# Softmax probabilities multiplied by inverted row sums on GpSimd, ahead of transposes that run two rounds behind the scores

## What is computed

```python
h = layernorm(x) * (1 + ca) + sa
x = x + ga * attention(h)      # 16 heads of 64
h = layernorm(x) * (1 + cb) + sb
x = x + gb * experts(h)        # 160 experts of 64, 8 kept per token, and a shared one

# attention, for each batch and head
scores = q @ k.T / 8 + bias          # 512 x 512, bias by relative position
attn = softmax(scores, axis=-1)
a = attn @ v
y = concat(a over heads) @ o_w.T
```

## Time and profile before

| what | value |
|---|---|
| median of 3 runs | 1040.71 us (1038.21 to 1040.87) |
| profiled execution: its time, its span | 1039.4 us, 1037.6 us |
| TensorE matmuls busy | 974.3 us, 94% |
| VectorE, ScalarE, GpSimd busy | 770.4 us (74%), 696.6 us (67%), 20.0 us (2%) |
| exponentials on ScalarE (L747) | 256, 718 ns each |
| biased scores on VectorE (L1028) | 256, 688 ns each |

### The profile page before, as it was taken

One profiled execution on the slowest core, in us unless ns is written; L12 is line 12 of the kernel. 1 busy time (PEld: TensorE's weight loads), 2 busy tenths in 40 slices (PEclk: granted clock), 3 DMA queues, 4 the chain that ended last, 5 costly groups with the idle time before them and its releaser, 6 DMA issues.

```text
span 1037.6 us, 16983 instructions
## 1 busy us (share of the span) xinstructions
PE 974.3 (94%) x4720; PEld 704.8 (68%) x4720; DVE 770.4 (74%) x1356; ACT 696.6 (67%) x1200; POOL 20.0 (2%) x36
## 2 busy tenths in 40 slices
PE   4899999999999999999978699999999999999997
PEld 2565656566666666666643487888888888888886
DVE  5766656566566665666655488999999999999997
ACT  4556656566665666666645567777777777777775
POOL 0000000000000000000000000000000000000000
PEclk9999999999999999999998899999999999999999
DMA  7874353443543534534500499999999999999992
GB/s 211 270 200 107 80 140 82 103 108 80 137 106 78 122 88 115 122 82 102 122 21 1 135 219 221 220 218 220 219 217 222 219 219 219 220 218 221 219 219 66
DMA packets 71106, 160.49 MB, mean 155 GB/s; under 512 B 10272, under 2 KB 36192, under 8 KB 60944
## 3 DMA queue, kind: packets, MB, share of 16 engines
q1 hardware_dynamic: 71056, 159.97, 68.3%
HBM read 105.60 MB, written 2.42 MB: 104 GB/s over the span
## 4 chain that ended last, share of the span: by engine, by line
PE 86%; ACT 4%; DMA 3%; DVE 3%; issue 2%; SPq 2%; DVEq 0%; ACTq 0%
PE ps L658 41%; PE ps L466 11%; PE ps L451 9%; PE ps L434 5%; PE ps L436 5%; PE ps L408 4%; PE ps L419 2%; PE ps L487 2%; PE ps L479 2%; ACT r_sb L762 2%; DMA k_low<-qk 1%; DMA hcur<-hT 1%; SPq L298 1%; DMA comb_rows<-strips 1%; PE ps L576 1%
## 5 line engine op out<-in xcount | busy, mean ns | idle before, releaser
L747 ACT ACTIVATE prob<-s_sb,nmax 128x512 f32<-128x512 f32 x256 | 183.6, 718 | 114.1 <-DVE nmax L1028 113.5
L658 PE MATMUL ps<-hT,wT 128*128 128x512 f32 x960 | 244.6, 391 | 0.3 <-DVE wT L1191 0.3
L1210 DVE TENSOR_TENSOR PT<-v_sb,strips 128x1024 f32<-128x1024 f32 x160 | 195.8, 1224 | 43.2 <-ACT v_sb L879 29.7
L658 PEld LDWEIGHTS ps<-hT,wT 128*128 128x128 f32 x960 | 180.8, 189 | 39.1 <-ACT strips L854 1.1
L658 PE MATMUL ps<-stack,wT 128*128 128x512 f32 x640 | 198.3, 392 | 9.0 <-DVE wT L1197 9.0
L879 ACT ACTIVATE v_sb<-ps 128x1024 f32<-128x1024 f32 x160 | 164.4, 1028 | 60.1 <-PE ps L658 59.8
L229 DVE COPY PT<-ps 128x512 f32<-128x512 f32 x128 | 88.3, 690 | 145.2 <-PE ps L451 145.0
L1197 DVE TENSOR_TENSOR wT<-PT,stack 128x1024 fp32r<-128x1024 f32 x160 | 194.8, 1218 | 0.0
L871 ACT CAST stack<-PT 128x1024 fp32r<-128x1024 f32 x160 | 166.7, 1042 | 9.0 <-DVE PT L1210 9.0
L1028 DVE CUSTOM_DVE_ANT_0 s_sb<-ps,strips 128x512 f32<-128x512 f32 x256 | 166.8, 688 | 6.6 <-PE ps L436 6.5
L451 PE MATMUL ps<-ident,prob 128*128 128x128 f32 x1024 | 140.9, 275 | 12.0 <-ACT r_sb L762 8.7
(11 more groups left out here) (108 smaller groups left out, 758.4 us busy)
## 6 DMA issues: line engine op xcount, KB each, us to landing
strips<-comb_rows SPq DMA_DIRECT2D x158, 512.0 KB, 13.2
stack<-qk SPq DMA_DIRECT2D x128, 256.0 KB, 3.8
k_low<-qk SPq DMA_DIRECT2D x64, 128.0 KB, 3.7
hT<-qk SPq DMA_DIRECT2D x64, 128.0 KB, 3.7
strips<-bias_rows SPq DMA_DIRECT2D x3, 1792.0 KB, 10.2
strips<-in_L_ffn_w_gate SPq DMA_DIRECT2D x80, 64.0 KB, 11.6
strips<-in_L_ffn_w_down SPq DMA_DIRECT2D x80, 64.0 KB, 13.6
strips<-bias_rows SPq DMA_DIRECT2D x2, 896.0 KB, 5.2
```

Source lines behind the costliest of these rows:

```text
L658: last = nc.tensor.matmul(ps[:, bank + c, :], weights(a), rows(m, c), start=start and k == 0, stop=stop and k == 2, skip_group_check=True)
L747: nc.scalar.activation(prob[:, u % 4, :], s_sb[:, u % 2, :], ACT.Exp, bias=nmax[:, u % 4:u % 4 + 1], scale=-1.0, accum_out=rsum[:, n % 2, ...
L1210: nc.vector.tensor_tensor(weighted[:, k % 4, :], silu[:, k % 2, :], cb[:, r, half * HALF:(half + 1) * HALF], ALU.mult).then_inc(s_mul, 1)
```

## The change

- The sums are used on the probabilities. `invert_sums` runs for two units at a time (four times a pair), and GpSimd's new `normalise` multiplies each unit's prob in place by its column of rinv. `widen_sums`, `spread_sums`, `copy_sums`, r_sb and rinv_wide are gone. VectorE's multiply behind attend becomes `copy_o`, a plain copy.
- prob has eight buffers, one for each unit; `add_bias` writes its result there and `exponential` works in place. s_sb is gone.
- The transposes of two units stand two rounds behind their scores. `attend` for a pair, `project_out`, `project_v` and the copies move accordingly. `qk_high` and `qk_low` of pair n+2 now stand in round 3 of pair n, in front of the next pair's operations.
- Without the sums' transposes the two banks alternate with the unit's number, and `transpose_users` is gone.

```diff
-            def transpose_probs(b, n, u, final):
-                pe.wait_ge(s_exp, b * G + (UNITS * n + u + 1))
-                bank = bank_for(b, ("T", n, u), final)
+            def transpose_probs(b, n, u):
+                g = UNITS * n + u
+                pe.wait_ge(s_prob, b * G + (g + 1))
+                if g >= 2:
+                    pe.wait_ge(*copied(b, g - 2))
                 for kb in range(QT):
-                    last = nc.tensor.transpose(ps[:, bank, kb * P:(kb + 1) * P],
-                                               prob[:, u % 4, kb * P:(kb + 1) * P], ident[:, :])
+                    last = nc.tensor.transpose(ps[:, BANK_T + u % 2, kb * P:(kb + 1) * P],
+                                               prob[:, u, kb * P:(kb + 1) * P], ident[:, :])
                 last.then_inc(s_t, 1)
...
-            def spread_sums(b, n, final):
-
-                pe.wait_ge(s_wide, b * HPAIRS + (n + 1))
-                bank = bank_for(b, ("R", n, 0), final)
-                for qt in range(QT):
-                    last = nc.tensor.transpose(ps[:, bank, qt * P:(qt + 1) * P], rinv_wide[:, qt, :], ident[:, :])
-                last.then_inc(s_t, 1)
-
...
                 scores(b, n, 0)
                 scores(b, n, 1)
                 if n >= 2:
-                    project_out(b, n - 2)
+                    attend(b, n - 2, 2)
+                    attend(b, n - 2, 3)
                 if n == 0:
                     project_qk(b, 1)
                 if n >= 1:
-                    transpose_probs(b, n - 1, 6, final)
-                    transpose_probs(b, n - 1, 7, final)
+                    transpose_probs(b, n - 1, 4)
+                    transpose_probs(b, n - 1, 5)
 
                 scores(b, n, 2)
                 scores(b, n, 3)
-                if n >= 1:
-                    attend(b, n - 1, 0, final)
-                    attend(b, n - 1, 1, final)
-                    spread_sums(b, n - 1, final)
-                transpose_probs(b, n, 0, final)
-                transpose_probs(b, n, 1, final)
-
-                scores(b, n, 4)
-                scores(b, n, 5)
-                if n >= 1:
-                    attend(b, n - 1, 2, final)
-                    attend(b, n - 1, 3, final)
                 if n == 0:
                     project_v(b, 0)
                 if not (final and n >= HPAIRS - 1):
                     project_v(b, n + 1)
-                transpose_probs(b, n, 2, final)
-                transpose_probs(b, n, 3, final)
+                if n >= 2:
+                    project_out(b, n - 2)
+                if n >= 1:
+                    transpose_probs(b, n - 1, 6)
+                    transpose_probs(b, n - 1, 7)
+
+                scores(b, n, 4)
+                scores(b, n, 5)
+                if n >= 1:
+                    attend(b, n - 1, 0)
+                    attend(b, n - 1, 1)
+                transpose_probs(b, n, 0)
+                transpose_probs(b, n, 1)
 
                 scores(b, n, 6)
                 scores(b, n, 7)
@@ -533,8 +492,8 @@
                     transpose_y(b)
                 if not (final and n >= HPAIRS - 2):
                     project_qk(b, n + 2)
-                transpose_probs(b, n, 4, final)
-                transpose_probs(b, n, 5, final)
+                transpose_probs(b, n, 2)
+                transpose_probs(b, n, 3)
...
-                if n >= 1 or u >= 4:
-                    number, _, _ = tables[False][1]["T", n - (u < 4), (u + 4) % UNITS]
-                    act.wait_ge(s_t, b * NU + (number + 1))
-                nc.scalar.activation(prob[:, u % 4, :], s_sb[:, u % 2, :], ACT.Exp, bias=nmax[:, u % 4:u % 4 + 1],
-                                     scale=-1.0, accum_out=rsum[:, n % 2, u:u + 1]).then_inc(s_exp, 1)
+                nc.scalar.activation(prob[:, u, :], prob[:, u, :], ACT.Exp, bias=nmax[:, u:u + 1],
+                                     scale=-1.0, accum_out=rsum[:, u:u + 1]).then_inc(s_exp, 1)
 
             def copy_probs(b, n, u):
-                number, _, _ = tables[False][1]["T", n, u]
-                act.wait_ge(s_t, b * NU + (number + 1))
-                if u == ACT_COPIES[0] and n >= 2:
+                act.wait_ge(s_t, b * G + (UNITS * n + u + 1))
+                if u == 0 and n >= 2:
                     act.wait_ge(s_pv, b * HPAIRS + (n - 1))
...
             def pair(b, n, final=False):
 
+                exponential(b, n, 0)
+                exponential(b, n, 1)
+                if n == 0:
+                    qk_high(b, 1)
                 if n >= 1:
                     copy_probs(b, n - 1, 4)
-                exponential(b, n, 0)
-                exponential(b, n, 1)
+
+                exponential(b, n, 2)
+                exponential(b, n, 3)
+                if n == 0:
+                    copy_v(b, 0)
+                if not (final and n >= HPAIRS - 1):
+                    copy_v(b, n + 1)
                 if n >= 1:
                     copy_probs(b, n - 1, 6)
-                if not (final and n >= HPAIRS - 1):
-                    qk_high(b, n + 1)
-
-                exponential(b, n, 2)
-                if n >= 1:
-                    copy_sums(b, n - 1, final)
-                exponential(b, n, 3)
-
-                copy_probs(b, n, 0)
+
                 exponential(b, n, 4)
                 exponential(b, n, 5)
                 if n == 0:
-                    copy_v(b, 0)
                     first_high(2)
                     first_high(3)
-                if not (final and n >= HPAIRS - 1):
-                    copy_v(b, n + 1)
-
-                copy_probs(b, n, 2)
+                copy_probs(b, n, 0)
+
                 exponential(b, n, 6)
                 exponential(b, n, 7)
+                if not (final and n >= HPAIRS - 2):
+                    qk_high(b, n + 2)
+                copy_probs(b, n, 2)
...
-            def widen_sums(b, n):
-
-                pool.wait_ge(s_rinv, b * HPAIRS + (n + 1))
-                if n >= 1:
-                    number, _, _ = tables[False][1]["R", n - 1, 0]
-                    pool.wait_ge(s_t, b * NU + (number + 1))
-                pool.sem_inc(apart, 1)
-                nc.gpsimd.tensor_copy(rinv_wide[:, :, :].rearrange("p q (h d) -> p q h d", h=2),
-                                      rinv[:, n % 2, :].rearrange("p (h q o) -> p q h o", h=2, o=1).broadcast_to(
-                                          [P, QT, 2, HD])).then_inc(s_wide, 1)
-
-            widen_sums(0, 0)
-            with pool.Fori(0, B - 1) as b:
-                for n in range(1, HPAIRS + 1):
-                    widen_sums(b, n)
-            for n in range(1, HPAIRS):
-                widen_sums(B - 1, n)
+            def normalise(b, n, u):
+
+                if u % 2 == 0:
+                    pool.wait_ge(s_rinv, b * (G // 2) + (UNITS * n + u) // 2 + 1)
+                    pool.sem_inc(apart, 1)
+                nc.gpsimd.tensor_scalar(prob[:, u, :], prob[:, u, :], rinv[:, u:u + 1], None,
+                                        ALU.mult).then_inc(s_prob, 1)
+
+            with pool.Fori(0, B) as b:
+                for n in range(HPAIRS):
+                    for u in range(UNITS):
+                        normalise(b, n, u)
...
                 g = UNITS * n + u
                 dve.wait_ge(s_s, b * G + (g + 1))
-                if g >= 2:
-                    dve.wait_ge(s_exp, b * G + (g - 1))
+                if g == UNITS - 1:
+                    dve.wait_ge(grp_used, 2)
+                if n >= 1:
+                    dve.wait_ge(s_t, b * G + (g - UNITS + 1))
                 dve.sem_inc(apart, 1)
                 if u == 0 and 2 * n in STRIP_PARTS:
                     dve.wait_ge(ld[f"strips{STRIP_PARTS.index(2 * n)}"], 16)
                 at = strip3[:, 2 * (n % HPAIRS) + head, qt * P:qt * P + S]
                 backwards = bass.AP(at.tensor, at.offset + S - 1, [list(at.ap[0]), [-1, S]])
-                nc.vector.tensor_tensor_reduce(out=s_sb[:, u % 2, :], in0=ps[:, BANK_S + u % 2, :],
+                nc.vector.tensor_tensor_reduce(out=prob[:, u, :], in0=ps[:, BANK_S + u % 2, :],
                                                in1=backwards, scale=-1.0, scalar=3.0e38,
                                                op0=ALU.add, op1=ALU.min,
-                                               accum_out=nmax[:, u % 4:u % 4 + 1]).then_inc(s_ttr, 1)
+                                               accum_out=nmax[:, u:u + 1]).then_inc(s_ttr, 1)
 
             def copy_probs(b, n, u):
-                number, _, _ = tables[False][1]["T", n, u]
-                dve.wait_ge(s_t, b * NU + (number + 1))
+                dve.wait_ge(s_t, b * G + (UNITS * n + u + 1))
                 if u == 1 and n >= 2:
                     dve.wait_ge(s_pv, b * HPAIRS + (n - 1))
-                copy_unit(nc.vector.tensor_copy, n, u, number).then_inc(s_cd, 1)
-
-            def invert_sums(b, n):
-                dve.wait_ge(s_exp, b * G + UNITS * (n + 1))
```

(55 more changed lines are left out.)

82 lines of the change are left out of this document (25 added, 57 removed).

## The result

The changed kernel took 1014.8 us in the median (1013.8 to 1015.6, four runs), the kernel before 1040.8 beside it: a ratio of 0.976 with an interval of 0.974 to 0.977, 26 us less. The forecast was 1013, so the total came out within 2 us. It did so by luck, with terms that missed in both directions, and the multiply, which was priced without a row, cost more than its upper bound. TensorE's matmuls are busy for 953.2 us (94%), VectorE 769.4 (76%), ScalarE 679.4 (67%), GpSimd 398.1 (39%, it was 2%).

A forecast was written before the change was run, and what follows sets the result against it. TensorE was taken to bound the attention stage, pair by pair. From the profiled 1039.4 us, 27.0 (pairs) and 8.1 (DMAs) off and 7.2 (seams) back gave 1011.5, or 1013 against the median; range 999 to 1030.

The forecast's parts named there:

- TensorE sets the pair: In the attention stage TensorE's work sets the time, one pair of heads at a time, 32 times, 15.27 us each before.
- R: TensorE's transposes of the widened sums; removing them and the wait they bring was priced at 1.04 us a pair.
- A's new wait of 0.4: In each pair the first attend waits about 0.4 us for ScalarE's copy of probabilities, making a pair 14.4 us.
- the rival of TensorE's full pace: In the attention stage attend's wait vanishes or ScalarE comes early enough: a pair at 14.0, 1001 us, chance 0.14.
- The 0.23 read as a wait: In each pair of the kernel before, TensorE was taken to wait 0.23 us before the first attend.
- The multiply at 1.0 between 0.62 and 1.23: GpSimd's multiply of 128x512 was priced at 1.0 us, bounds 0.62 and 1.23; eight a pair, 8.0 us, hidden behind TensorE.
- The slow-multiply rival: GpSimd's multiplies set the pair if each takes 1.8 us or more; at 2.0 the time is 1055 us, chance 0.12.
- hcur: In the attention stage TensorE's waits for the load of hcur go: 4.8 us, plus 1.7 us of slow clock.
- k_low: In the attention stage TensorE's 1.6 us wait for a stack's DMA goes, as qk_low moves about two rounds earlier.
- the head: The first pairs of the attention stage, whose extra cost was left at nothing.
- The seams: At three seams between batches, longer waits behind VectorE's queue and a slower clock give back 7.2 us together.
- The end: The tail behind the last scores was left at nothing: more work there but fewer waits.

The follow-up runs named there:

- sums_free: The kernel before in its old order, without widening, transposes and copy of the sums or the multiply by them, so without the division: 1014.3 us, ratio 0.978.
- cheap_pool: The changed kernel with GpSimd's multiply replaced by a copy in place, so without the division by the sums: 1013.6 us, ratio 0.973.
- lag_one: The changed kernel with transposes one round behind their scores, engine orders shifted to match, reciprocals right behind the biased scores: 1098.3 us, ratio 1.055.
- strips_late: The changed kernel with bias strips 3 and 4 loaded one stack later each: four runs of 1011.0, 1016.9, 1031.4 and 1034.3 us, no ratio.

## Why the prediction came out right

**TensorE sets the pair: right.** Taking R out was worth 1.03 in sums_free, priced at 1.04; the parts behind this agree less well (see there).

**A's new wait of 0.4: wrong, 6.7 us too pessimistic over 28 pairs.** The chain was followed with each record's full duration, but records of one engine overlap a little. ScalarE in the changed kernel, round 1 and 2 of the pair whose scores start at 228.73:

```profile
234.94 0.71 ACT L706 ACTIVATE prob<-prob,nmax 128x512 f32<-128x512 f32 x1
235.55 0.19 ACT L706 ACTIVATION_READ_ACCUMULATOR prob<-prob,nmax 128x1 f32 x1
235.64 0.56 ACT L719 COPY v_sb<-ps 128x512 f32<-128x512 f32 x1
236.11 0.58 ACT L204 COPY PT<-ps 128x512 f32<-128x512 f32 x1
```

copy_v starts at 6.91 behind the pair's start where I had 7.25, and it takes 0.47 from start to start, not 0.55. The copy of unit 6 ends at 7.96 instead of 8.3, and A starts at 8.27, which is 1.10 behind its S, the distance that it has without any wait. qk_high, likewise, was 0.90 in pace (228.65 to 229.55) against 1.01 in length, and a reciprocal 0.07 against the 0.20 charged for it. From the 14.01 of the prediction to the 14.17 measured it is then 0.09 more for S in front of each A, 0.05 more for T behind each A and 0.10 less for v, which took 0.71 instead of 0.81. No wait is in it: for the pair the rival of TensorE's full pace came true, and the forecast's step of a late copy in front of A failed. The 0.23 read as a wait in the kernel before was likewise 0.13, since 1.10 is the bare distance.

**The multiply at 1.0 between 0.62 and 1.23: the price was wrong, its cover right.** It is 1.56. The bounds came from the engine's own copy, 0.62, and twice that; the product with a scalar from memory is 2.5 copies. The slow-multiply rival needed 1.8 to decide; the real margin was 0.2 us an operation (14.17 over 8 is 1.77), not the 0.8 that the forecast gave itself. Of the rivals I had given this one 0.12, which the price turned out nearly to earn. The two rounds of lag made latency free in the steady pairs (cheap_pool, lag_one), though not in the tail (see the end, below).
The estimate from the Trainium skill (GPSIMD Engine Reference, "Performance versus the Vector engine"), 1.35 us, was nearer than mine and still low. The page's ratio was measured on an add of two tiles, not on a product with a column. Against VectorE on the same operands in SBUF the ratio measured here is 1.56 to 0.48, 3.2 and not 1.96.

**hcur: right.** 6.6 us against 6.5, and sums_free shows that it was the order that removed it, since without the new order the waits grew from 4.8 to 8.5. The forecast asked for both moves, and lag_one bears it out: with qk_low early but `project_v` in its old round, SP waits up to 6.1 us for `project_v` and the matmuls wait 4.2 us for hcur.

**k_low: wrong, and the head with it.** The 1.6 us wait was to go, because qk_low comes two rounds earlier. SP does issue pair 2's stack 3.8 us earlier (46.04, before 49.88), but its transfers share the DMA engines with two strips of 1.8 MB issued in front of them and land no earlier, while TensorE arrives sooner (at 59.0, before 60.6). The wait is now 3.8. strips_late shows the cause: with the second of them behind the stack the wait is gone and pairs 1 and 2 take 3.2 less. The whole stretch up to pair 3 missed its forecast by 5.4 us. Of this 1.0 lies in front of the first scores, which start at 29.4 (before 28.4, and 28.0 to 29.4 in the other profiles with the same order in the attention); its cause is open.

**The seams: right in kind, 2.6 us too small.** TensorE's waits were 4.5 where 4.1 was forecast, for the jump took 3.88 on VectorE and not the 2.73 of the earlier trace rows; part of the difference was absorbed, since VectorE came to it 3.9 us behind the pair's start and not 4.2. I had taken idle time measured in one order as the price of the jump; how much of it is a fixed cost no row of before could tell. The clock fell behind both waits. Beside the waits 3.0 and 2.1 us are left (7.5 and 6.6 less 4.5) against 1.7 each; the granted clock of 0.52 and 0.69 over 5.5 us stands for 2.6 and 1.7 of them. The third seam, without a jump, cost 1.5 against 1.4. By the rule of the Trainium skill (TensorE: Matmul & The Clock Gate, "What's actually happening") a wait of this length need not be caught; here both were, 0.52 and 0.69 in the windows shown.

**The end: 1.1 us longer, forecast at nothing.** The tail of the attention is what grew. From the start of pair 31 to the last `project_out` it was 21.7 us before (540.07 less 518.33) and is 23.9 now (515.61 less 491.68); with the copy in cheap_pool it is 22.3. So 1.6 of these 2.2 us are the multiply, which has no round of scores to hide behind there:

```profile
509.68 0.65 PE L420 MATMUL ps<-ident,prob 128*128 128x128 f32 x4 [0.88 <-POOL prob L859]
```

The prediction gave the tail "more work behind the last scores but fewer waits"; the waits were not fewer, 2.5 us of TensorE's up to the last `project_out` against 2.0 before. The stages behind the tail were about 1 us shorter in this profile, which the edit doesn't explain.

**The sum** was right since +6.7 for the pairs met -2.6, -5.4 and -1.1 for seams, head and end. Each of these four is a miss of its own, and that their balance, 2.3 us, is small is luck.

## What to carry to other kernels

Follow a chain across engines by start-to-start differences of records, not by their durations: 0.1 us at each of four steps was the whole forecast wait. An operation on an idle engine is free up to its share of the period, and its latency is free if its reader stands far enough behind (but not at the ends, where there is nothing to hide it); here that lag came before the engine's speed. Before work is moved to the place where an engine jumps back, look at what the jump costs: here writing out the loops brought 12 us on top of the change's 26.

## What the hardware showed that I had not expected

- GpSimd multiplies 128x512 floats by a column in 1.56 us (1.54 back to back) and copies them in 0.62. VectorE does the product in 0.48 when both sides are in SBUF, and a copy out of PSUM in 0.69.
- A jump back costs VectorE 3.9 us of idle time in the changed order, 2.7 in the order before and 4.5 in lag_one, so it is no constant; what sets it stays open. Writing all loops out saved 12 us.
- S in front of A takes 1.10 us and otherwise 1.01, T behind A 0.85 and behind a projection 0.80, with the multiply, with a copy in its place and with GpSimd idle (sums_free).
- The same expert stage ran at 213 or 222 GB/s in different executions and kernels, 3 to 8 us apart, without a change to it.
